# Semaphores of a stage cleared by TensorE in the head of the next stage, no block of their own

## The reference

```python
edge_index = jnp.stack([src, dst])
h = jnp.maximum(_layernorm(x, axis=-1), 0.0)
x = x + _L0_gnn_ref(h, edge_index, ...)                # attention, softmax over the edges of dst, tanh
h = jnp.maximum(_layernorm(x, axis=-1), 0.0)
x = x + _L1_gnn_ref(h, edge_index, edge_attr_16, ...)  # four heads, batch norm over all nodes, gelu
h = jnp.maximum(_layernorm(x, axis=-1), 0.0)
x = x + _L2_gnn_ref(h, edge_index, edge_attr_18, ...)  # q, k, v; softmax over the edges of src
h = jnp.maximum(_layernorm(x, axis=-1), 0.0)
x = x + _L3_gnn_ref(h, edge_weight, ..., src, dst, edge_type_3)  # two rounds of messages, GRU, batch norm
return x
```

## Time and profile before

| | us |
|---|---|
| median of 3 runs | 6562.67 (6551.64 to 6565.39) |
| the profiled execution, its own time | 6559.05 |
| its span, from the first to the last instruction | 6557.2 |
| busy in the span: PE, PEld | 4111.0, 2125.2 |
| busy in the span: DVE, ACT, POOL | 4689.3, 3313.6, 4496.8 |

### The profile page before, as it was taken

The page is one execution under the profiler, slowest core; times in us unless marked ns, Lnnn a source line. Parts: engine busy times, 40 slices in busy tenths (PEclk is TensorE's granted clock), DMA queues, the critical chain, the costliest instruction groups (busy, mean ns, idle before and its releaser), DMA issues. The chain is left out here.

```text
span 6557.2 us, 85933 instructions
## 1 busy us (share of the span) xinstructions
PE 4111.0 (63%) x15111; PEld 2125.2 (32%) x15111; DVE 4689.3 (72%) x9073; ACT 3313.6 (51%) x5670; POOL 4496.8 (69%) x4877
## 2 busy tenths in 40 slices
PE   0101555555489997899976777765777677777600
PEld 0000211111144443666643333332444344444300
DVE  5884888888689998666745555555777676666667
ACT  1111444444367775788866666665777533333200
POOL 4777888888766663655648888886666477777733
PEclk9999999999999998899978888887999887788755
DMA  2442222222266665999944444442333233333378
GB/s 86 137 152 57 79 76 76 76 73 75 64 160 173 172 173 144 165 190 192 196 103 118 111 116 113 111 118 70 80 78 79 58 71 70 70 71 69 67 310 315
DMA packets 949965, 773.07 MB, mean 118 GB/s; under 512 B 661200, under 2 KB 727709, under 8 KB 945876
## 3 DMA queue, kind: packets, MB, share of 16 engines
q1 hardware_dynamic: 819859, 614.72, 32.0%
q0 software_dynamic: 125504, 131.83, 13.3%
q10 hardware_dynamic: 4512, 25.60, 1.0%
HBM read 472.43 MB, written 310.28 MB: 119 GB/s over the span
## 5 line engine op out<-in xcount | busy, mean ns | idle before, releaser
L205 ACT ACT_TABLE_LOAD x621 | 796.7, 1283 | 139.4 <-PEq L66 128.9
L918 POOL DMA_INDIRECT l_rows<-x,l_num x392 | 444.3, 1133 | 148.8 <-issue 93.6
L954 POOL DMA_INDIRECT x<-l_out,l_snum x392 | 472.4, 1205 | 106.5 <-issue 90.0
L954 POOL DMA_INDIRECT m<-l2s_out,l2s_snum x392 | 437.6, 1116 | 151.2 <-issue 105.5
L1159 POOL DMA_INDIRECT pre_src_rows<-in_x,all_idx_src x392 | 397.4, 1014 | 164.5 <-issue 130.4
L918 POOL DMA_INDIRECT l_rows<-in_x,l_num x392 | 432.0, 1102 | 105.8 <-issue 90.7
L918 POOL DMA_INDIRECT l3a_rows<-m,l3a_num x392 | 397.7, 1014 | 144.8 <-issue 93.5
L918 POOL DMA_INDIRECT l2s_rows<-vc_rows,l2s_num x392 | 417.3, 1065 | 106.3 <-issue 95.2
L918 POOL DMA_INDIRECT l_rows<-eo,l_num x392 | 386.3, 985 | 147.5 <-issue 96.4
L954 POOL DMA_INDIRECT xg<-l3b_out,l3b_snum x392 | 394.9, 1007 | 111.8 <-issue 90.6
L918 POOL DMA_INDIRECT l3b_rows<-g_rows,l3b_num x392 | 386.2, 985 | 106.3 <-issue 92.1
(11 more groups left out here) (407 smaller groups left out, 13621.4 us busy)
## 6 DMA issues: line engine op xcount, KB each, us to landing
l_far<-far_d SPq DMA_DIRECT2D x196, 256.0 KB, 3.7
xg<-l2s_bg_row SPq DMA_DIRECT2D x97, 512.0 KB, 3.8
dl_xin<-xg SPq DMA_DIRECT2D x31, 1600.0 KB
l2s_bg_x<-x SPq DMA_DIRECT2D x97, 260.0 KB, 3.1
x<-ts_row SPq DMA_DIRECT2D x31, 812.5 KB, 4.4
l_keep<-keep_d SPq DMA_DIRECT2D x196, 128.0 KB
xs<-l_xT SPq DMA_DIRECT2D x98, 256.0 KB
hs<-l_hT SPq DMA_DIRECT2D x98, 256.0 KB, 3.1
```

Source lines behind the costliest of these rows:

```text
L205: act.add_instruction(mybir.InstLoadActFuncSet(name=nc.get_next_instruction_name(), ins=[], outs=[], act_func_set_id=which))
L918: pool.indirect_dma_start(self.buf[k.q][:, j, at:at + w], None, table, bass.IndirectOffsetOnAxis(ap=self.num[k.q][:, m, j:j + 1], axis=0)) ...
L954: pool.indirect_dma_start(self.table, bass.IndirectOffsetOnAxis(ap=self.num[k.q][:, j:j + 1], axis=0), self.out[k.q][:, j, 0:self.cols], N ...
```

## The change

A stage's semaphores are no longer cleared in a block behind it. `Scope.__exit__` only notes them in `Scope.left`, and keeps their numbers from being given away (`sem_stack`, `kept_back`); in the next stage's block the TensorE function begins with `Scope.clear_left(pe)`, which clears what is noted, and at that stage's exit the numbers become free. dl gets a TensorE function that does only this. The outermost scope, at the end, clears what is left (dl's) in a block on POOL, as each scope did before.

```diff
--- before.py
+++ after.py
@@ -52,9 +52,11 @@
 
 
     def __init__(self, nc, name):
-        self.nc, self.name, self.stack, self.used = nc, name, ExitStack(), []
+        self.nc, self.name, self.stack, self.sem_stack, self.used = nc, name, ExitStack(), ExitStack(), []
 
     whole = None
+
+    left, kept_back, cleared = [], [], []
 
     def __enter__(self):
         self.stack.__enter__()
@@ -62,13 +64,30 @@
 
     def __exit__(self, *a):
 
-        if self.used and a[0] is None:
-            with self.nc.Block() as block:
-                @block.gpsimd
-                def _(pool):
-                    for s in self.used:
-                        pool.sem_clear(s)
+        if a[0] is None:
+            for stack in Scope.cleared:
+                stack.close()
+            Scope.cleared.clear()
+            Scope.left.extend(self.used)
+            Scope.kept_back.append(self.sem_stack)
+            if self is Scope.whole:
+                with self.nc.Block() as block:
+                    @block.gpsimd
+                    def _(pool):
+                        Scope.clear_left(pool)
+                for stack in Scope.cleared:
+                    stack.close()
+                Scope.cleared.clear()
         return self.stack.__exit__(*a)
+
+    @staticmethod
+    def clear_left(eng):
+
+        for s in Scope.left:
+            eng.sem_clear(s)
+        Scope.cleared.extend(Scope.kept_back)
+        Scope.left.clear()
+        Scope.kept_back.clear()
 
     def sb(self, name, shape, dt=F32):
         return self.stack.enter_context(self.nc.sbuf_tensor(f"{self.name}_{name}", shape, dt))
@@ -77,7 +96,7 @@
         return self.stack.enter_context(self.nc.psum_tensor(f"{self.name}_{name}", list(shape), F32))
 
     def sem(self, name):
-        s = self.stack.enter_context(self.nc.semaphore(f"{self.name}_{name}"))
+        s = self.sem_stack.enter_context(self.nc.semaphore(f"{self.name}_{name}"))
         self.used.append(s)
         return s
 
@@ -425,6 +444,7 @@
 
             @block.tensor
             def _(pe):
+                Scope.clear_left(pe)
                 n = 0
 
                 def flip(psum, rows):
@@ -2431,6 +2459,10 @@
         stored = [s.sem(f"stored{u}") for u in range(2)]
         done, dve_step, pool_done = s.sem("done"), s.sem("dve_step"), s.sem("pool_done")
         with nc.Block() as block:
+            @block.tensor
+            def _(pe):
+                Scope.clear_left(pe)
+
             @block.sync
             def _(sp):
                 def body(k):
```

## The result

| | before | after |
|---|---|---|
| median of 8 runs, us | 6564.75 (6551.64 to 6571.48) | 6543.20 (6538.45 to 6563.38) |
| the profiled execution | 6559.05 | 6538.45 |
| its span | 6557.2 | 6536.7 |

The ratio of after to before is 0.9974, with a 95% interval from 0.9963 to 0.9984: 17 us faster by the ratio (10 to 24 by its interval), 21.5 by the medians, 20.5 by the spans.

A forecast was written before the change was run, and what follows sets the result against it. Barriers make the time a plain sum of stages and pauses; 22.0 us removed less 0.7 in q gives 21.3, so 6537.8 from the profiled time or 6541.4 from the median; predicted 6540 us, range 6530 to 6552.

The forecast's parts named there:

- The time is a plain sum, the pauses are 22.0 us: Ten stages cut by barriers, nothing overlapping; the clearing pieces at nine places between them, 22.0 us, are removed.
- PE's clear costs 0.12 us, between 0.063 and 0.2: Price of each of 287 clears on PE, 0.12 us from PE's satisfied semaphore waits; ends 0.063 and 0.2.
- q loses 0.7: Head of q: 6 clears on PE, 0.7 us, with a cover of only 0.05 us, counted wholly as lost.
- Hidden in prep, l0, l1, l2, l2s, l3a, l3b, dl: Heads of these stages: PE's clears run beside waits for gathers or other engines' steps and cost nothing.
- the covers: How late PE's clears may make a stage's first work: q 0.05, l1 8.3, l2 12.3, l2s 8.5, l3b 5.5 us.
- Code supply costs nothing: Clearing blocks as pauses for fetching code: their loss put at nothing, though moved code blocks add to the range.
- The first rival, PE's clock: Gain given back in the stages by PE's clock or moved code, 9 us or more; 6554 us; chance 0.15.
- The row for l2s: Profile row cited for the clock rival: in l2s granted clock 0.82, PE busy 816 of 1168 us.
- The second rival: Heads of q, l1, l2, l2s, l3b: dear PE clears make it slower, decided from 0.3 us each; chance 0.04.
- The sum: Whole kernel: 22.0 us removed less 0.7 lost in q, a gain of 21.3 us; 17.7 with dear clears.
- the 13 us (0.2%) that the forecast set as its mark: Whole kernel: about what a measurement can tell from no change; faster by over 0.2% had chance 0.80.

The follow-up runs named there:

- before_again: The kernel before, run once more with no edit; 6577.28 us in one execution.
- before_ranges: The kernel before with its clearing blocks kept, but POOL clears each row of neighbouring semaphores with one instruction; ratio 0.9976 (0.9964 to 0.9988).
- after_ranges: The changed kernel, but TensorE clears each row of neighbouring semaphores with one instruction; ratio 0.9968 (0.9956 to 0.9981) to before.
- after_third: The changed kernel measured once more, unedited, on the chip of warm; 6555.09 us, ratio 0.9963 (0.9948 to 0.9978) to before.
- after_empty_blocks: The changed kernel with the further block behind each scope kept, holding one POOL instruction that does nothing; 6535.78 us in one execution.
- pause_l3b: The changed kernel with the old clearing block on POOL put back between l3a and l3b; 6566.74 us in one execution.
- after_x4: The changed kernel with each semaphore cleared four times over by TensorE; ratio 1.0036 (1.0020 to 1.0051) to before.

## Why l3b became longer

The trace of before and that of after, 19.2 us into l3b (PE; start, us, engine, line, count), first before:

```profile
5206.71 2.12 PE L2409 MATMUL l3b_p_gate<-all_w_gate,l3b_acc 128*128 128x256 f32 x8
```

```profile
5189.27 3.35 PE L2437 MATMUL l3b_p_gate<-all_w_gate,l3b_acc 128*128 128x256 f32 x8
```

The same eight products take 2.12 us in the one and 3.35 in the other. The granted clock differs there. The first 25 us of l3b, again before, then after (the last but two is the granted clock):

```profile
5187.51:5212.51 25.00, 13.36 (x36) 6.38 (x36) 7.85 (x19) 4.60 (x8) 19.30 (x25) 0.61 0.38 54
```

```profile
5170.08:5195.08 25.00, 14.55 (x36) 7.23 (x36) 7.17 (x16) 4.19 (x7) 19.28 (x25) 0.56 0.38 55
```

0.61 against 0.56: of 25 us at 1.2 or 2.4 GHz, PE had the high level for 5.4 us before, from 19.6 us into the stage on, and for 2.9 after, from 22.1 on. By my estimate 2.5 us more at half speed can cost at most 1.2 us. VectorE's first work on the third chunk comes that much later, first before, then after:

```profile
5212.27 0.76 DVE L2357 TENSOR_TENSOR l3b_hm<-l3b_rows,l3b_w 128x256 f32<-128x256 f32 x2
```

```profile
5196.05 0.76 DVE L2384 TENSOR_TENSOR l3b_hm<-l3b_rows,l3b_w 128x256 f32<-128x256 f32 x2
```

That is 24.8 us into the stage against 26.0. At the ninth chunk after is 2.5 us behind (87.9 against 85.4), at the 81st 1.5 (831.6 against 830.1). So the lengthening of l3b arises in its first 90 us; what adds to the clock's 1.2 us there isn't shown.

In before, before_again and before_ranges the clock of the first 25 us was 0.60 or 0.61, in all profiles of the changed kernel and its variants, but for warm below, 0.56 or less. I took the pause itself for the cause: the clock falls at the end of l3a, and a stage that starts 2.8 us sooner has more of the low stretch inside it. before_ranges already spoke against it: behind l3a it has a pause of only 0.5 us, and still the clock has 0.60 and l3b takes 1050.8 us.

```diff
-            if self is Scope.whole:
+            if self is Scope.whole or self.name == "l3a":
```

> The changed kernel, with the old clearing block on POOL put back at one place, between l3a and l3b. In two executions of before and one of before_ranges l3b took 1049.8 to 1051.1 us, in four with the block gone 1052.1 to 1053.7; the rows show products at L2409 that run at half speed some 2 us further into the stage, and TensorE's granted clock is low until 22 us after the stage's start instead of 20. My theory: the clock fell at the end of l3a and rises a given time later, so a stage that starts 2.8 us sooner has 2 us more of it; with the pause back l3b takes 1050 to 1051 us and the low stretch ends 20 us into it. The rival (something else in the changed program, the places of the code or of the semaphores, lengthens l3b): 1052 to 1054 us and 22 us also with the pause. The time between the stages is 2.8 us.

The first 25 us, and all of l3b:

```profile
5192.85:5217.85 25.00, 14.70 (x36) 7.22 (x36) 6.63 (x15) 4.19 (x7) 19.30 (x25) 0.55 0.39 55
...
5192.85:6246.65 1053.80, 754.77 (x2752) 434.20 (x2752) 704.45 (x1480) 320.80 (x592) 825.03 (x980) 0.80 0.34 68
```

That theory fails. With the pause back (one execution, 6566.74 us; 2.5 us between l3a and l3b, less than the 2.8 expected) the clock still has 0.55, and l3b takes 1053.8 us, where 1050 to 1051 were expected. The rival's forecast (1052 to 1054 us) came true, in this one execution: something else in the changed program goes with the longer l3b. The clock's records say a little more. In before it fell 7.7 us ahead of l3b's start and rose 27.3 us later; in after it fell 5.2 us ahead and rose 27.3 us later too; with the pause back it fell 8.0 us ahead, as in before, but rose only after 30.7 us. That the low clock costs l3b time rests on the rows of PE and VectorE above, on the third chunk of this run (26.4 us into the stage, late like the clock), and on the run warm, below. Why the clock rises later in every variant of the changed kernel but warm, even with the pause, stays open.

Whether the clock's rise can be brought forward was the last experiment:

```diff
+def warm(pe, c, p, n):
+
+    for _ in range(n):
+        pe.matmul(p, c.ident[:], c.ident[:], start=True, stop=True)
...
                 Scope.clear_left(pe)
                 stat.begin(pe, c)
+                warm(pe, c, p_score[:, 0:P], 8)
...
                 Scope.clear_left(pe)
+                warm(pe, c, p_back[:, 0:P], 16)
```

(and 16 each in l2s and l3b, on top of after_ranges; the products go into memory that the first real work overwrites.)

> The kernel of after_ranges with idle products of TensorE put in the heads of l1 (8), l2, l2s and l3b (16 each), 128 by 128 by 128, whose results nobody reads: some 7 us of work ahead of the first gathered rows, which come after 8.5 to 13.6 us. My theory: TensorE's clock rises sooner in those stages, so the early products run at full speed: l3b 2 to 3 us shorter than in the changed kernel (1050 us), l2s up to 3 us shorter, l1 1 us; 4 to 6 us together, 0.9960 of before. The rival (the clock rises at its own time whatever TensorE does in the head, or the early products are not on the path): all stages as in after_ranges, 0.9968; if the idle products come in the way of the first real ones, l2s and l3b are 1 to 2 us longer.

> The changed kernel once more, as the measure for warm on the same chip. My theory: 21 us faster than before, ratio 0.9968, within 0.1%; q 9.9 us, l3b 1052 to 1053 us. The rival (the gain of the first measurement was partly the chip's): over 0.999.

Measured on the same chip: the changed kernel 6555.09 us, ratio 0.9963 (0.9948 to 0.9978), 27 us faster than before, so the gain isn't one chip's; warm 6547.43 us, ratio 0.9939 (0.9921 to 0.9956), 35 us faster than before and 8 than the changed kernel, more than the 4 to 6 expected. All four runs of warm lie below all seven of the changed kernel. Of the 8 us, 0.6 are q's and come from the shortened clears; after_ranges itself was not run on this chip. First after_third's l2s and l3b, then warm's l2s, the first 25 us of its l3b, and all of it:

```profile
3340.08:4500.13 1160.05, 808.52 (x2940) 390.31 (x2940) 649.28 (x1176) 723.64 (x985) 898.94 (x982) 0.83 0.40 109
...
5181.72:6233.50 1051.78, 761.61 (x2752) 429.96 (x2752) 704.45 (x1480) 320.80 (x592) 823.98 (x980) 0.80 0.34 68
```

```profile
3342.50:4497.36 1154.86, 805.99 (x2972) 393.39 (x2972) 649.19 (x1176) 723.99 (x985) 901.56 (x982) 0.84 0.40 110
...
5179.27:5204.27 25.00, 17.45 (x76) 11.79 (x76) 10.32 (x23) 4.92 (x9) 19.30 (x25) 0.84 0.37 55
...
5179.27:6227.93 1048.66, 761.85 (x2784) 434.31 (x2784) 704.31 (x1480) 320.96 (x592) 823.53 (x980) 0.80 0.34 68
```

The idle products took 5.7 us in l2s and 6.6 in l3b:

```profile
3343.53 5.74 PE L246 MATMUL l2s_p_score<-all_ident 128*128 128x128 f32 x32 [7.16 <-PEq L1662]
...
5181.45 6.63 PE L246 MATMUL l3b_p<-all_ident 128*128 128x128 f32 x32
```

The granted clock of the first 25 us of l3b is 0.84 in place of 0.56, and l3b takes 1048.7 us, the shortest of all; its third chunk comes at 21.9 us in place of 26.0. In l2s the clock has 0.84 in place of 0.50, and the stage takes 1154.9 us, where the two other profiles on that chip have 1160.1 and 1160.5. The row transposes of its fourth chunk, first after_third's, then warm's, show that the whole lead is there after some 40 us (42.5 against 37.2 us into the stage):

```profile
3382.53 1.06 PE L2016 MATMUL l2s_p_vT<-all_ident,l2s_rows 128*68 128x128 f32 x4
```

```profile
3379.68 1.06 PE L2036 MATMUL l2s_p_vT<-all_ident,l2s_rows 128*68 128x128 f32 x4
```

l1 and l2 show no gain. The Trainium skill (TensorE: Matmul & The Clock Gate, section Part 1: The HAM clock gate) says that activity of PE releases its throttle; warm agrees with it, 0.84 against 0.56.

## The prediction, point by point

- *The time is a plain sum, the pauses are 22.0 us.* Right: 22.1 in two executions, all of it gone. The working from rounded starts was 0.1 off.
- *PE's clear costs 0.12 us, between 0.063 and 0.2.* Right: 0.119. The Trainium skill (Runtime: NRT & Kernel Launch, section The launch sequence) puts the runtime's own reset of 51 semaphores an engine at about 1.5 us, by estimate some 29 ns for one; neither PE's 119 nor POOL's 63 ns agree with it, and the measurement decides.
- *q loses 0.7.* Right: 0.78, and 2.9 with four times the clears, as by its cover of nothing.
- *Hidden in prep, l0, l1, l2, l2s, l3a, l3b, dl.* Right as to the covers: the first row work is where it was, and gives way by the computed amounts, to 1.4 us, when the clears are made dear. What the covers don't say is how much of a late start reaches a stage's end: nearly all in l2, l2s and l3b, a part in l1.
- *Code supply costs nothing.* No stage but l3b is longer without its pause, and neither the short pauses of after_empty_blocks nor the long one of pause_l3b made a stage shorter. prep is 0.8 us shorter than before without a reason that I know; that stays open.
- *The first rival, PE's clock.* It was named for l2s as a draw, up to 8 us either way. In l2s there was nothing to be told apart. l3b, which the prediction didn't name, became 1.6 us longer every time; the clock's later rise there accounts for some 1.2 us by estimate, and why it rises later is open. The row for l2s also holds the 3.4 us of clears behind l2, which changes nothing in the working. In l0 the clock was another surprise, below.
- *The second rival* needed 0.3 us a clear. after_x4 makes it real with 0.48 us: 27 us slower than before, where the same covers gave 34. Its price never arose in the change itself.
- *The sum.* 22.1 - 0.8 (q) - 1.6 (l3b) + 0.8 (prep) = 20.5 us, which is the difference of the spans; 21.3 were forecast. That two stages moved unforeseen, l3b and prep, and nearly made up for each other, is luck, and so is that the other stages' wandering cancelled in that pair (l2 +4.8, dl -3.0, l0 -2.1). The timed runs don't resolve the sum to a microsecond: by the interval the gain is 10 to 24 us, and its lower end is under the 13 us (0.2%) that the forecast set as its mark. The forecast of 6540 against 6543.2 is off by 3.2 us, most of which is the choice of the starting point between the profiled time and the median: from the median of three runs it would have been 6541.4, from that of eight (6564.75) 6543.5.

## What to carry to other kernels

Where stages end in barriers, look at what runs between them: its price is plain to read, and here the next stages took back only some 2 us of 22. Housekeeping belongs on the engine with the longest wait at a stage's start, not on the one that does it fastest: PE at 0.12 us a clear hides what POOL at 0.06 doesn't (17 to 27 us gained against 4, on different chips). Before moving it, ask whether it can be said in fewer instructions; 28 clears of rows of semaphores took away nearly three quarters of the time between the stages (16.0 of 22.1 us) with the old structure.

## What the hardware showed that I hadn't expected

PE's clock, and where it matters. l0 ran at full clock in the first profile and almost wholly at the lower level in after_ranges (granted clock 1.00 and 0.51), first before, then after_ranges:

```profile
616.68:1794.07 1177.39, 604.78 (x1176) 217.28 (x1176) 947.66 (x1960) 507.62 (x1177) 956.42 (x981) 1.00 0.27 74
```

```profile
613.07:1793.12 1180.05, 602.32 (x1176) 217.36 (x1176) 947.25 (x1960) 507.56 (x1177) 958.76 (x981) 0.51 0.27 74
```

Its length differs by 2.7 us of 1180, no more than between runs: PE works 605 us of it and is waited for little. In l2s and l3b, on the other hand, 5.7 and 6.6 us of idle products in the head of the stage, which do nothing but keep PE at work, were worth some 5 and 3 us. So a mean clock (0.900 for before, 0.838 for after) says nothing of a kernel's time until one knows in which stage it fell.
